# First batch's routing drawn forward, more of its row transfers in the first program, six matmuls left out

## The chip, the cores and the metric

One core of one Trainium2 chip. The time is device microseconds (us) of one launch. The kernel before ran in 748.58 us, the median of three runs (748.47 to 749.82).

## The reference, cut to what matters

One transformer block over x of 2 batches x 1024 tokens x 256, in float32:

```python
h = layernorm(x) * (1 + ca) + sa                 # ca, sa, ga, ... from silu(c) @ wmod, per batch
x = x + ga * attention(h)                        # 32 heads of 8, 8 key heads, causal softmax, then @ wo
h = layernorm(x) * (1 + cb) + sb
probs = softmax(h @ w_router)                    # 16 experts
top_w, top_i = top_k(probs, 4); top_w /= sum(top_w)
moe = sum over the 4 chosen e of top_w[e] * (silu(h @ we1[e]) * (h @ we3[e])) @ we2[e]      # H = 128
shared = (silu(h @ ws1) * (h @ ws3)) @ ws2                                                  # 512 wide
x = x + gb * (shared / 5 + moe * 4 / 5)
```

## The kernel before, in words

The kernel is two programs one after the other. Each is a block of instruction lists, one for each engine, and an engine starts the second block only when all engines have come to the end of the first.

**The first program** makes the projections and then the attention in 16 groups (batch x key head), each in 10 steps (`STEPS`, s = 0 to 9). TensorE (PE) computes the scores of step s in one or two slots into PSUM banks (L1264), ScalarE (ACT) takes their exponentials (L1047, L1052), GpSimd (POOL) zeroes what the causal mask hides in the steps s = 0, 1, 2, 7, 8, 9 (L871), and PE multiplies with the values two steps later (`product`, L1283). VectorE (DVE) works out row maxima for the group after (L1453 and others). They end in group 14 of 0 to 15, since the maxima run ahead; in the rest of group 14 and in group 15 DVE is free.

The first batch (groups 0 to 7) is out of the attention early, so its second half is laid into the groups of the other batch: output projection in group 13 (`output_pair`), layernorm moments after it, and, once DVE has done its last maxima, `normal(1)`, `normal(2)` (L212). From there `first_batch(group, s)`, called at the end of each step of PE's list, places: `turned_x(1)`, `turned_x(2)` (transposes, L518) after steps 6 and 7 of group 14, `router(1)`, `router(2)` (logits, L534) after steps 8 and 9 of it, and `ranks` (two products that count hits per expert, L280 and L281) after step 4 of group 15. DVE makes from the transposed rows `h2` (L1533), its high part `h2_hi` (L1536) one column block at a time, and its low part (L1541), then the routing (`Routing`): `logits` (L240, L241), a wait for ACT's exponential of the logits (L1031, placed ahead of step 1 of group 15), `best`, `best_at`, `chosen`, `counted` (L248 to L266: it releases `ranks`), `weights`, and, once `ranks` is done, `totals`, `firsts`, `places`, which end with the row positions `posi` (L309, semaphore `pos_ready`).

Every token's row goes to 4 sorted places in memory: 32 indirect transfers (`scatter(pool, 0, k)`, 128 rows each, L549) issued by POOL. Transfer 0 stands ahead of the mask of step 8 in group 15 (`AMONG`), 1 to 7 behind the mask of step 9, some behind waits (`spread`, `att_full`, `up1_full`) that pace them, and 8 to 31 at the start of the second program.

After the attention's last product PE does `reciprocals`, `output(3)` (L577) and `up(0)`, `up(1)`, the first two products of the shared expert (L605), and the first program ends.

**The second program.** SP starts the loads of all experts' weights (`w_all`, L1613 and L1614), and behind them, once all 32 transfers have landed (`sorted_s[0]`), the loads of the sorted rows by tiles of 128 (L1622). PE goes through `reciprocals(4)`, `output(4)`, `down(0)` to `down(3)` (L1796), `up(2)` to `up(4)`, `turned_x(3)` and `(4)`, `router(3)` and `(4)` (L534), then six products of the identity that nobody reads (L1869), and then the loop over 94 tiles: `turned_rows` (L1809), `up_rows` (L1830), `turned_g` (L1841), `down_rows` (L1847). `turned_rows(0)` waits for the first tile's load and for DVE's `shared_mult(4)` (L1907). ACT's list ahead of the loop ends with `high(4)` (L1707), the exponential of the second batch's logits (L1760) and one small Silu (L1762) that brings the table for the loop; then come `shifted_rows(0)` and `(1)` (L1729). Behind the loop is the rest of the shared expert, and the outputs.

The order on each engine is written out by hand. There is no planner.

## Time and profile before

| | |
|---|---|
| median of three runs | 748.58 us |
| span of the profiled execution (first to last instruction) | 745.6 us, 3.0 us under that median |
| PE busy | 696.8 us, 93% |
| DVE, ACT, POOL busy | 72%, 66%, 37% |
| mean granted TensorE clock | 0.972 of full |
| POOL, 32 transfers of the first batch's rows (L549) | 30.7 us, 959 ns each |

All times are on the profile's own clock, from the first instruction. A busy engine can still be waiting in effect: PE has 93% here, and what counts is where it stands idle and what it then waits for. The attention ends near 478 us and the first program near 487.9 us. Of the granted clock, 1.00 is 2.4 GHz and 0.50 is 1.2 GHz.

### The profile page before, as it was taken

The numbers are of one execution on the slowest core, as the hardware profiler recorded it, in microseconds if no ns is written. First come the engines' busy times: TensorE is split into PE (matmuls) and PEld (weight loads), VectorE is DVE, ScalarE is ACT, GpSimd is POOL, SyncE is SP. The second block draws the span as 40 slices with busy tenths as digits, with TensorE's granted clock in tenths as the row PEclk, the third lists the DMA queues.
The fourth block names the chain that finished last, engine by engine and source line by source line (L and its number), as shares of the span: only waits on it lengthen the run. The fifth ranks groups of instructions, "written<-read, shape, count | busy, mean of one in ns | idle before, by whom it ended". The sixth has DMA issues, their size and how long they took to land. (4 is left out here: it accounts for less than half of the span.)

```text
span 745.6 us, 14744 instructions
## 1 busy us (share of the span) xinstructions
PE 696.8 (93%) x4960; PEld 441.5 (59%) x4960; DVE 539.0 (72%) x1159; ACT 493.6 (66%) x739; POOL 272.2 (37%) x332
## 2 busy tenths in 40 slices
PE   8989899999999999999999888897899999999994
PEld 7447544444445444444444434577678888887883
DVE  7846988888888888888887775456395556775477
ACT  4341579999898988899888477345556666664232
POOL 5702104433323222233332112567016706540772
PEclk9998989999999999999999999997799999999999
DMA  7755603455453554543443000387447758873342
GB/s 234 204 119 148 183 5 105 116 161 166 156 167 100 162 159 142 161 106 103 116 124 87 1 19 30 110 267 254 128 148 249 267 178 235 245 235 129 92 140 79
DMA packets 78580, 108.71 MB, mean 146 GB/s; under 512 B 16200, under 2 KB 60040, under 8 KB 77420
## 3 DMA queue, kind: packets, MB, share of 16 engines
q1 hardware_dynamic: 67996, 77.16, 35.6%
q0 software_dynamic: 9280, 29.11, 12.1%
q10 hardware_dynamic: 1232, 1.51, 0.7%
q8 instruction: 42, 0.69, 0.4%
q14 instruction: 30, 0.25, 0.1%
HBM read 59.92 MB, written 47.39 MB: 144 GB/s over the span
## 5 line engine op out<-in xcount | busy, mean ns | idle before, releaser
L1052 ACT ACTIVATE probs<-psum 128x1024 f32<-128x1024 f32 x256 | 246.6, 1027 | 47.2 <-PE psum L1264 46.7
L1453 DVE TENSOR_REDUCE max_parts<-psum 128x2 f32<-128x1024 f32 (+2 forms) x160 | 196.0, 1225 | 68.1 <-PE psum L1200 66.3
L871 POOL TENSOR_SCALAR_AFFINE_SELECT probs<-probs 128x512 f32<-128x512 f32 (+1 forms) x96 | 79.2, 826 | 221.1 <-ACT probs L1052 201.5
L1283 PE MATMUL psum<-probs,v_aug 128*32 128x512 f32 (+3 forms) x1536 | 158.9, 501 | 0.3 <-POOL probs L871 0.2
L1264 PE MATMUL psum<-qs,ks 64*128 64x512 f32 (+3 forms) x768 | 136.2, 394 | 11.5 <-ACT over L978 5.0
L1264 PEld LDWEIGHTS psum<-qs,ks 64*128 64x128 f32 x768 | 65.8, 186 | 109.7 <-ACT probs L1052 69.0
L1830 PE MATMUL psum<-w_all,v_aug 128*128 x376 | 98.7, 386 | 0.7 <-ACT v_aug L1729 0.6
L1200 PE MATMUL psum<-km,qs 64*128 64x128 f32 (+2 forms) x608 | 75.6, 322 | 8.4 <-DVE max_parts L1453 4.2
L1729 ACT ACTIVATE v_aug<-psum,modc 128x128 f32<-128x128 f32 x188 | 75.7, 453 | 4.9 <-PE psum L1809 4.6
L1830 PEld LDWEIGHTS psum<-w_all,v_aug 128*128 128x128 f32 x376 | 71.9, 193 | 11.6 <-issue 2.0
L1283 PEld LDWEIGHTS psum<-probs,v_aug 128*32 128x32 f32 x1536 | 34.0, 109 | 65.5 <-issue 61.2
L1927 DVE TENSOR_TENSOR v_aug<-v_aug,psum 128x128 f32<-128x128 f32 x94 | 27.0, 287 | 60.7 <-ACT v_aug L1737 60.6
L1212 PE MATMUL psum<-km,qs 64*128 64x512 f32 x160 | 66.0, 413 | 0.4 <-DVE max_parts L1472 0.2
L1737 ACT ACTIVATE v_aug<-psum 128x128 f32<-128x128 f32 x94 | 26.0, 277 | 58.3 <-PE psum L1830 58.3
L1200 PEld LDWEIGHTS psum<-km,qs 64*128 64x128 f32 x608 | 51.1, 187 | 19.1 <-DVE max_parts L1453 10.3
L1847 PE MATMUL psum<-w_all,v_aug 128*128 x188 | 56.5, 383 | 0.0
L978 ACT ACTIVATE over<-psum 128x1024 f32<-128x1024 f32 x48 | 49.3, 1026 | 10.5 <-DVE max_parts L1472 5.1
L1659 POOL DMA_INDIRECT h_t<-y_sorted,posi x32 | 31.5, 985 | 55.3 <-PE psum L605 23.7
L549 POOL DMA_INDIRECT x_sorted<-probs,posi x32 | 30.7, 959 | 46.5 <-DVE posi L309 34.3
L1472 DVE CUSTOM_DVE_ANT_0 psum<-psum,over 128x512 f32<-128x512 f32 x64 | 44.2, 691 | 0.0
L1809 PE MATMUL psum<-ident,late 128*128 128x128 f32 x188 | 36.8, 279 | 6.5 <-DMA late<-x_sorted 6.5
L1940 DVE TENSOR_TENSOR late<-psum,gate 128x256 f32<-128x256 f32 x94 | 39.5, 421 | 1.2 <-PE psum L1847 1.0
(200 smaller groups left out, 1014.6 us busy)
## 6 DMA issues: line engine op xcount, KB each, us to landing
late<-x_sorted SPq DMA_DIRECT2D x94, 128.0 KB, 2.8
y_sorted<-late SPq DMA_DIRECT2D x94, 128.0 KB
x_sorted<-g_rows POOLq DMA_DIRECT2D x6, 1536.0 KB, 7.4
qs<-q_parts SPq DMA_DIRECT2D x62, 128.0 KB
km<-k_parts SPq DMA_DIRECT2D x62, 96.0 KB
km<-k_parts SPq DMA_DIRECT2D x64, 64.0 KB
ks<-k_parts SPq DMA_DIRECT2D x64, 64.0 KB
y_sums<-g_sign SPq DMA_DIRECT2D x16, 256.0 KB, 2.7
```

The lines of the kernel that those rows point to most:

```text
L871: pool.affine_select(out=tile, in_=tile, compare_op=ALU.is_ge, fill=0.0, base=0, pattern=[[0, REP], [0, n], [1, P]], channel_multiplier=-1 ...
L978: act.activation(to, psum[:, banks, :], ACT.Relu).then_inc(over_done, 1)
L1052: act.activation(to[:, 2 * slot:2 * slot + 2, off:TT], psum[:, banks, off:TT], ACT.Exp, scale=SCALE).then_inc(p_full, 1)
L1200: last = pe.matmul(bank[wide_bank + hp][:, k * w:(k + 1) * w], qs[buf][rows, hh, i * P:(i + 1) * P], km[buf][rows, at:at + w], start=(k == ...
L1212: pe.matmul(bank[narrow_bank][:], qs[buf][rows, hh, i * P:(i + 1) * P], km[buf][rows, KU:KU + TT], start=True, stop=True).then_inc(narrow_ ...
L1264: last = pe.matmul(bank[first + hp][:, to:to + width], ks[buf][rows, c * P:(c + 1) * P], qs[buf][rows, hh, half * TT + off:(half + 1) * TT ...
L1283: last = pe.matmul(bank[sum_bank][32 * h:32 * h + 32, off:TT], v_aug[:, at:at + 32], probs[(NSTEP * group + s) % (LAG + 1)][:, h, col:col ...
L1453: dve.tensor_reduce(out=max_parts[:, :, h0:h1, slice(*tiles), slot], in_=psum[:, wide_bank:wide_bank + 2, :].rearrange("p a (s w) -> p (a ...
L1472: dve.tensor_tensor_reduce(out=bank[narrow_bank][:], in0=bank[narrow_bank][:], in1=over[:, hp, :], scale=1.0, scalar=LEAST, op0=ALU.add, o ...
L1729: last = act.activation(xt[:, k % 2, c * P:(c + 1) * P], bank[X_BANKS[k % 2]][:, c * P:(c + 1) * P], ACT.Identity, scale=modc[:, b, 1, c, ...
L1830: last = pe.matmul(bank[U_BANKS[k % 2]][:, 0:2 * H], xt[:, k % 2, c * P:(c + 1) * P], w_all[:, bass.ds(expert[k], 1), c * 2 * H:(c + 1) * ...
L1847: pe.matmul(bank[Y_BANKS[k % 2]][:, 0:D], gt[:, k % 2, :], w_all[:, bass.ds(expert[k], 1), W13:WCOLS].rearrange("p a n -> p (a n)"), start ...
```

## The change

Seven edits:

1. On PE, `turned_x(1)`, `turned_x(2)`, `router(1)`, `router(2)` stand one step earlier in group 14 (after steps 5, 6, 7, 8), and `ranks` after step 0 of group 15 instead of step 4. `router` for the first batch waits for `xt2_read`, which counts the `h2` pieces, and the semaphore `h2_dve` is gone.
2. On DVE the high part is made for 1024 columns at a time (`high_parts`), once ahead of the logits and once ahead of `best`; the low part (`low_parts`) moves behind `places`.
3. ACT's exponential of the first batch's logits stands between the two slots of step 9 in group 14.
4. POOL's transfers 0 to 4 stand ahead of the mask of step 7 of group 15, transfer 5 ahead of that of step 8, and 6 to 14 behind the mask of step 9, with the waits that 1 to 7 had.
5. In the second program 17 transfers are left (15 to 31) instead of 24, and the waits between them are dealt out anew; the last four come behind `down_done` 2.
6. The six identity products (L1869) are gone.
7. A semaphore less is allocated.

```diff
@@ -424,8 +424,8 @@
         wo_done, yn_pool, yn_dve, att_full = sem("wo_gated_done"), sem("yn_by_pool"), sem("yn_by_dve"), sem("att_full")
         var2, sqrt2, xn2_done = sem("var2_ready"), sem("sqrt2_done"), sem("xn2_done")
         resid, xt2_full, xt2_read = sem("residual_done"), sem("xt2_full"), sem("xt2_read")
-        h2_dve, h2_act, hi_dve, hi_act, h2_lo_s, h2_lo1_s = [sem(n) for n in (
-            "h2_by_dve", "h2_by_act", "h2_high_by_dve", "h2_high_by_act", "h2_low_done", "h2_low1_done")]
+        h2_act, hi_dve, hi_act, h2_lo_s, h2_lo1_s = [sem(n) for n in (
+            "h2_by_act", "h2_high_by_dve", "h2_high_by_act", "h2_low_done", "h2_low1_done")]
         lg_full = sem("logits_full")
         lg_banks = 6, 5
 
@@ -522,7 +522,7 @@
         def router(pe, n):
             half, to = (n - 1) % 2, bank[lg_banks[(n - 1) // 2]]
             if n <= 2:
-                pe.wait_ge(h2_dve, DC * n)
+                pe.wait_ge(xt2_read, DC * n)
                 if n == 1:
                     pe.wait_ge(narrow_free, NPAIR * GROUPS)
             else:
@@ -537,8 +537,8 @@
 
         sorted_s = [sem(f"x_sorted_{b}") for b in range(B)]
 
-        AMONG = {8: (0,)}
-        SCATTERED = 8
+        AMONG = {NSTEP - 3: range(5), NSTEP - 2: range(5, 6)}
+        SCATTERED = 15
 
         def scatter(pool, b, k):
 
@@ -906,16 +906,17 @@
                             pool.wait_ge(y_in[n], 64)
                             pool.tensor_tensor(out=y_t[0][:, n], in0=y_t[0][:, n], in1=r_t[:, n], op=ALU.mult).then_inc(yn_pool, 1)
 
-                scatter(pool, 0, 1)
+                scatter(pool, 0, 6)
                 for m in range(DC):
                     pool.wait_ge(spread, m + 1)
-                    scatter(pool, 0, 2 + m)
-                scatter(pool, 0, 4)
+                    scatter(pool, 0, 7 + m)
+                scatter(pool, 0, 9)
                 pool.wait_ge(att_full, 5)
-                scatter(pool, 0, 5)
-                scatter(pool, 0, 6)
+                scatter(pool, 0, 10)
+                scatter(pool, 0, 11)
                 pool.wait_ge(up1_full, 1)
-                scatter(pool, 0, 7)
+                for k in range(12, SCATTERED):
+                    scatter(pool, 0, k)
 
             @block.scalar
             def _(act):
@@ -1026,9 +1027,6 @@
                     for s, (half, blocks, n) in enumerate(STEPS):
                         if group == GROUPS - 2 and s == 3:
                             square_roots(act, 0, var2, sqrt2)
-                        if group == GROUPS - 1 and s == 1:
-                            act.wait_ge(lg_ready, 1)
-                            act.activation(route[0].lg, route[0].lg, ACT.Exp).then_inc(lg_exp, 1)
                         if NSTEP * group + s > LAG:
                             act.wait_ge(pv_done, NSTEP * group + s - LAG)
                         if NSTEP * group + s == LAG:
@@ -1036,6 +1034,9 @@
                         to = probs[(NSTEP * group + s) % (LAG + 1)]
                         for slot in range(3 if (s, 2) in DIFF_AT else 2):
                             banks = banks_of(group, s, slot)
+                            if group == GROUPS - 2 and s == NSTEP - 1 and slot == 1:
+                                act.wait_ge(lg_ready, 1)
+                                act.activation(route[0].lg, route[0].lg, ACT.Exp).then_inc(lg_exp, 1)
                             if (s, slot) in DIFF_AT:
                                 which, ahead = DIFF_AT[s, slot]
                                 if group + ahead < GROUPS:
@@ -1304,11 +1305,11 @@
 
                     if group == OUT_GROUP and OUT_STEP <= s < OUT_STEP + 4:
                         output_pair(s - OUT_STEP)
-                    elif group == GROUPS - 2 and s in (6, 7):
-                        turned_x(pe, s - 5)
-                    elif group == GROUPS - 2 and s in (8, 9):
-                        router(pe, s - 7)
-                    elif group == GROUPS - 1 and s == 4:
+                    elif group == GROUPS - 2 and s in (5, 6):
+                        turned_x(pe, s - 4)
+                    elif group == GROUPS - 2 and s in (7, 8):
+                        router(pe, s - 6)
+                    elif group == GROUPS - 1 and s == 0:
                         route[0].ranks(pe, bank[lg_banks[0]][:, 2 * P:4 * P])
 
                 pe.wait_ge(v_done, 2)
@@ -1532,19 +1533,24 @@
                         dve.wait_ge(xt2_full, k)
                         dve.tensor_scalar(h2[:, n - 1, c, :], bank[T_BANKS[n - 1][c]][:], modc[:, 0, 1, c, 0:1],
                                           modc[:, 0, 1, c, 1:2], ALU.mult, ALU.add).then_inc(xt2_read, 1)
-                        dve.wait_ge(xt2_read, k)
-                        dve.tensor_copy(h2_hi[0][:, c, toks], h2[:, n - 1, c, :]).then_inc(hi_dve, 1)
-                        dve.sem_inc(h2_dve, 1)
-                for n in (1, 2):
+
+                def high_parts(n):
+                    toks = slice((n - 1) * TT, n * TT)
+                    dve.wait_ge(xt2_read, DC * n)
+                    dve.tensor_copy(h2_hi[0][:, :, toks], h2[:, n - 1]).then_inc(hi_dve, DC)
+
+                def low_parts(n):
                     toks = slice((n - 1) * TT, n * TT)
                     dve.wait_ge(hi_dve, DC * n)
                     dve.tensor_tensor(out=h2_lo[0][:, :, toks], in0=h2[:, n - 1], in1=h2_hi[0][:, :, toks].bitcast(F32),
                                       op=ALU.subtract).then_inc(h2_lo_s, 1)
 
+                high_parts(1)
                 dve.wait_ge(lg_full, 2)
                 route[0].logits(dve, chain.link, bank[lg_banks[0]][:, 0:P].rearrange("p (j e) -> p j e", e=E))
 
                 ranked = bank[lg_banks[0]][:, 2 * P:4 * P]
+                high_parts(2)
                 route[0].best(dve, chain.link)
                 route[0].best_at(dve, chain.link, range(TC))
                 route[0].chosen(dve, chain.link)
@@ -1553,6 +1559,8 @@
                 route[0].totals(dve, chain.link, ranked, range(TC))
                 route[0].firsts(dve, chain.link, ranked)
                 route[0].places(dve, chain.link)
+                for n in (1, 2):
+                    low_parts(n)
                 late_reciprocals(dve, 0)
                 spread_sums(dve, 0)
                 residual(dve, chain.link, 3)
@@ -1664,33 +1672,20 @@
                     for k in some:
                         scatter(pool, 0, k)
 
-                scatters(8, 9)
+                scatters(15, 16)
                 for m in range(DC):
                     pool.wait_ge(spread, DC + m + 1)
-                    scatters(10 + 2 * m, 11 + 2 * m)
+                    scatters(17 + 2 * m, 18 + 2 * m)
                 pool.wait_ge(up1_full, 3)
-                scatters(14, 15)
+                scatters(21, 22)
                 pool.wait_ge(up3_full, 3)
-                scatters(16, 17)
+                scatters(23, 24)
                 pool.wait_ge(att_full, 6)
-                scatters(18)
+                scatters(25)
                 pool.wait_ge(down_done, 1)
-                scatters(19, 20)
+                scatters(26, 27)
                 pool.wait_ge(down_done, 2)
-                scatters(21)
-                pool.wait_ge(up1_full, 4)
-                scatters(22)
-                pool.wait_ge(up3_full, 4)
-                scatters(23)
-                pool.wait_ge(down_done, 3)
-                scatters(24, 25)
-                for c in range(2 * DC):
-                    pool.wait_ge(xt2_full, 2 * DC + c + 1)
-                    scatters(26 + c)
-                pool.wait_ge(up1_full, 5)
-                scatters(30)
-                pool.wait_ge(up3_full, 5)
-                scatters(31)
+                scatters(28, 29, 30, 31)
                 for k in range(ROUTES):
                     if k:
                         pool.wait_ge(u_full, ROUTED_AT + 4 * k // 5)
@@ -1865,8 +1860,6 @@
                 router(pe, 4)
 
                 pe.wait_ge(hi_act, 2 * DC)
-                for _ in range(6):
-                    pe.matmul(bank[Y_BANKS[1]][:, 0:P], ident[:], ident[:], start=True, stop=True)
                 for i in range(-AHEAD_T, NTILE + 2):
                     if 0 <= i < NTILE:
                         up_rows(i)
```

## Rows read from the trace of the kernel before

**Rows 1.** The chain of waits, 487 to 526 us: start us, us, what.

```profile
519.71 2.39 DMA x_sorted<-xn,posi
...
522.12 2.03 DMA late<-x_sorted
```

**Rows 2.** The waits, 485 to 530 us: us in total, times, longest.

```profile
PE psum L1809 <- DMA late<-x_sorted: 6.5, 1, 6.5
```

**Rows 3.** The timeline of ACT: start us, us, what, [idle before <-releaser].

```profile
518.94 1.28 ACT L1762 ACT_TABLE_LOAD   x1
520.23 0.20 ACT L1762 ACTIVATE v_aug<-sd 128x1 f32<-128x1 f32 x1
524.92 1.50 ACT L1729 ACTIVATE v_aug<-psum,modc 128x128 f32<-128x128 f32 x4 [4.49 <-PE psum L1809]
```

**Rows 4.** The timeline of DVE in the second program.

```profile
515.96 0.68 DVE L1907 TENSOR_TENSOR wmod_sb<-wmod_sb,psum 128x512 f32<-128x512 f32 x1
```

**Rows 5.** The timeline of PE, the identity products.

```profile
514.82 2.91 PE L1869 MATMUL psum<-ident 128*128 128x128 f32 x12
```

**Rows 6.** The timeline of PE in groups 14 and 15.

```profile
440.96 0.50 PE L1264 MATMUL psum<-qs,ks 64*128 64x512 f32 x2 [0.41 <-ACT probs L1052]
...
449.41 0.79 PE L1264 MATMUL psum<-qs,ks 64*128 64x384 f32 x8
...
451.12 1.96 PE L534 MATMUL psum<-wr_sb,h_t 128*128 128x16 f32 x16
...
453.67 0.64 PE L1283 MATMUL psum<-probs,v_aug 128*32 128x256 f32 x8
...
462.56 0.49 PE L280 MATMUL psum<-wmod_sb,g_rows 128*128 128x128 f32 x2
```

**Rows 7.** The timeline of ACT in groups 14 and 15.

```profile
450.01 1.94 ACT L1052 ACTIVATE probs<-psum 128x1024 f32<-128x1024 f32 x2 [2.29 <-PE psum L1264]
...
455.43 0.31 ACT L1031 ACTIVATE g_rows<-g_rows 128x128 f32<-128x128 f32 x1
455.63 1.02 ACT L1047 ACTIVATE probs<-psum 128x1024 f32<-128x1024 f32 x1
...
463.80 3.77 ACT L1052 ACTIVATE probs<-psum 128x1024 f32<-128x1024 f32 x4 [0.40 <-PE psum L1264]
```

**Rows 8.** The timeline of DVE, the first batch's routing.

```profile
453.12 0.29 DVE L240 TENSOR_REDUCE g_rows<-psum 128x8 f32<-128x128 f32 x1 [2.15 <-PE psum L534]
...
455.89 0.71 DVE L248 MAX8 wmod_sb<-g_rows 128x8 f32<-128x16 f32 x8 [2.15 <-ACT g_rows L1031]
...
459.20 1.07 DVE L266 TENSOR_REDUCE wmod_sb<-wmod_sb 128x128 f32<-128x512 f32 x1
...
469.49 0.18 DVE L309 CAST posi<-wmod_sb 128x32 uint32<-128x32 f32 x1
```

**Rows 9.** The timeline of POOL at the end of the first program.

```profile
481.99 0.96 POOL L549 DMA_INDIRECT x_sorted<-xn,posi  x1 [2.18 <-PE psum L577]
...
488.51 0.96 POOL L549 DMA_INDIRECT x_sorted<-xn,posi  x1 [3.04 <-POOLq L634]
```

**Rows 10.** The timeline of PE across the two programs.

```profile
486.68 0.63 PE L605 MATMUL psum<-km,w_hi 128*128 128x512 f32 x2
488.91 2.05 PE L588 MATMUL psum<-k_parts_sb 128*128 128x128 f32 x16 [1.60 <-DVE k_parts_sb L612]
```

**Rows 11.** Stretches: us, PE, PEld, DVE, ACT, POOL busy (x), granted clock, DMA share, GB/s.

```profile
432.30:434.50 2.20, 0.06 (x6) 0.01 (x2) 0.94 (x3) 2.19 (x3) 0.00 (x0) 1.00 0.00 0
434.50:438.50 4.00, 4.00 (x25) 1.51 (x27) 2.85 (x8) 2.76 (x3) 0.33 (x2) 0.57 0.00 0
...
488.90:492.00 3.10, 3.09 (x22) 2.87 (x23) 1.51 (x3) 1.97 (x4) 2.49 (x3) 1.00 0.93 281
...
733.50:735.80 2.30, 0.10 (x2) 0.08 (x1) 1.60 (x4) 1.43 (x3) 0.00 (x0) 1.00 0.00 0
735.80:738.00 2.20, 1.61 (x12) 1.41 (x12) 2.06 (x6) 0.00 (x0) 0.00 (x0) 1.00 0.00 0
```

## The prediction

> **What bounds the kernel now.** I read the page first (busy shares, the granted clock by slices), then the chain that ended last, then the waits around the place where the chain leaves TensorE, and last the timelines of the engines there. PE is busy for 93% of the span, so the question is where it is not. The chain runs back from the end through the tile loop, all on PE, to one handover: the last indirect transfer of sorted rows starts on POOL at 519.71, lands 2.39 us later, the first tile's load takes 2.03 more, and PE's first transpose starts at 524.20 [rows 1]. The waits show that PE stood 6.5 us for that load [rows 2], the longest idle time in the whole trace. Ahead of it POOL is the chain: from 488.51 on it issues transfers 8 to 31 without a pause, 0.96 us each and 0.30 between, some of them slower. So the change aims at a real bound. How much it is worth depends on who is late next.
>
> **The change part by part.** I work on the profile's clock. Its span, 745.6, lies 3.0 under the median of the three runs, 748.58; I take differences and add them to the median.
>
> *The second program's transfers, 17 instead of 24.* At 1.26 us each, the seven that go would bring the last landing from 522.1 to 513 or before, and PE's other work ends at 514.82, where the identity products begin [rows 5]. If only transfers, tile load and PE counted, the loop would start near 515 and the gain would be 9 us. But two other lists end later. `turned_rows(0)` also waits for `shared_mult(4)` on DVE, which runs from 515.96 to 516.64 [rows 4]. And ACT, which must shift tile 0 before PE can multiply it, is still in its old list: the table load of the last Silu starts at 518.94 and the Silu itself ends at 520.43 [rows 3]. In the trace ACT's first shift is at 524.92 [rows 3]; after the change it is at 520.45 at the earliest, as everything in ACT's list up to there hangs on PE's and DVE's work and not on the transfers. The loop can therefore gain 524.92 − 520.45 = 4.5 us, half of the 9. Ends: 0, if the transfers, which then run wholly beside the weight loads, land only at 522; and 4.5, for the reason given. I take 4.5, since 17 transfers from 488.51 end by 510 to 511 and even a slow landing leaves several us.
>
> The Trainium skill (ScalarE: Activation LUTs, "What ACT_TABLE_LOAD costs") says that a switch of tables costs a drain of about the load's own length on top of the load. The trace has the Silu at 520.23, 0.01 behind the end of the load [rows 3], so nothing of the kind is seen at this switch. By the page, an ACT list with two switches would end 2.8 us later and the gain be 1.7; I follow the row.
>
> *The identity products.* They end at 517.73 and PE idles until 524.20 anyway [rows 2, 5]; the clock was at half all through them. What they hid is nothing; taken away they free PE for `turned_rows(0)`, which is ready at 516.7. Zero, with ends −0.5 and +0.5 (when the clock comes back after the restart).
>
> *The routing in groups 14 and 15.* `turned_x(1)` now fills PE's wait of 0.41 before 440.96 [rows 6]. `router(2)` comes ahead of step 9, so from 451.12 − 1.71 (the step that starts at 449.41 [rows 6]) − 0.4 and some tenths of overlap I put its start at 448.8 and the logits on DVE, which started 2.00 behind it [rows 6, 8], at 450.8. `lg_ready` is then at 451.4. ACT's exponential stands behind slot 0 of step 9. That slot started at 450.01 [rows 7]; behind `router(2)` instead of ahead of it, it starts at 451.2 and ends at 452.15. So the exponential is at 452.15, not 455.43 [rows 7], and doesn't wait. From exponential to `best` it was 0.46, and from `best` to the end of `counted` 459.20 + 1.07 − 455.89 = 4.4 [rows 8]. `hits_s` thus comes at 452.15 + 0.46 + 4.4 = 457.0. The two `high_parts` (0.9 each, an estimate from a cast of 512 columns at 0.43) fall into waits of DVE. `low_parts` are off every path there.
>
> Now the waiting place. PE used to come to `ranks` at 462.56 [rows 6], two us after `hits_s` at 460.3; it waited for nothing. In the new list `ranks` stands behind step 0 of group 15, whose product ended at 454.3 [rows 6] and will end at about 454.45 (0.6 of PE work less ahead of it, but slot 1 of its scores now waits for ACT's slot 1 of step 9, which the exponential pushed to 453.35). PE then stands 457.05 − 454.45 = **2.6 us** in front of `ranks`, and behind it in the list are the scores of step 1, for which ACT waits. Step 1 reaches ACT at 457.7 (end of `ranks`) + 0.5 = 458.2; it was 455.63 [rows 7]: +2.6. Of this 0.4 comes back at step 5, where `ranks` no longer delays the scores (ACT's idle 0.40 before 463.80 [rows 7]). From there to the end of the attention PE and ACT hand each other the work, ACT with hardly a gap, so that nothing more is regained: **+2.15 us** at the attention's end. Ends: +1.2 (`hits_s` an us sooner) and +3.2.
>
> *Transfers 0 to 4.* `posi` was written 469.49 − 462.56 = 6.9 us behind `ranks` [rows 6, 8]; now that is at 464.0. Five transfers from 464.2 at 1.26 to 1.6 us end at 470.5 to 472.2. The mask of step 7, behind them on POOL, could start at 470.2 and with the shift of 2.15 at 472.3. It isn't held up: 0, upper end +0.5. Transfer 5 stands where transfer 0 stood.
>
> *The end of the first program.* Transfer 10 waits for `att_full` 5 as transfer 5 did, at 481.99 [rows 9]. Then come five instead of two before the barrier: the last begins at 481.99 + 4 x 1.26 = 487.03 and ends at 487.99. PE's last product ends at 486.68 + 0.63 = 487.31 [rows 10]. So POOL takes PE's place as the last to arrive, by 0.7, or 1.0 with the 0.30 behind an issue. **+0.8 us**, between 0.4 and 1.2; all of the second program starts later by this. In the list behind it PE has no idle time from 488.91 on, so nothing absorbs it.
>
> Sum without the clock: −4.5 + 2.15 + 0.8 = **−1.5 us** (−1.55 rounded), 747.0.
>
> *The clock.* Both new waits touch it. After an idle time of 2.14 us in group 14 (PE busy 0.06 of 2.20) the granted clock was 0.57 in the 4.0 us behind it [rows 11]: 4.0 x 0.43 = 1.7 us of full-rate work lost. After 1.60 us between the programs [rows 10] it stayed 1.00 [rows 11], and after some 2.2 us near 733 too. So such a gap takes the clock sometimes. The stall in front of `ranks` (2.6 us, call it A) is in the attention, where the gap of 2.14 did; its price is 1.7, less some tenths that ACT hides: 1.4. The gap between the programs grows from 1.6 to 2.4 (B), and there PE is the bound and the price is the full 1.7. I hold A for more likely than not, B for even.
>
> The Trainium skill (TensorE: Matmul & The Clock Gate, "HAM oscillation") names as dangerous only gaps longer than any of these; by it neither A nor B would cost anything and the sum stays −1.5. The gap of 2.14 us with half clock behind it [rows 11] speaks against it, and the one near 733 for it.
>
> **The rivals.**
>
> 1. *Forecast: stall, later barrier and A.* −1.5 + 1.4 = −0.15: 748.4 us. No change that can be measured (0.2%, 1.5 us, is about what a measurement of this kernel can tell).
> 2. *A and B.* The wait in front of `ranks` and the longer gap both take the clock: −1.5 + 1.4 + 1.7 = +1.6, 750.1 us, slower. It decides from the point where POOL's end at the barrier makes PE's gap over two us. For it: 2.14 was enough once. Against: 1.60 in this very place wasn't, and 2.2 near 733 wasn't.
> 3. *No gap takes the clock* (what the page's rule gives too): 747.0 us, just faster.
> 4. *The stall in front of `ranks` isn't there*, because `hits_s` comes before PE or ACT has work in store: −4.5 + 0.8 and up to 0.4 lost or won: 744.9 us. Against it: from the exponential to `counted` are 4.9 us of DVE work in series, and PE has 2.3 us of work between the two.
> 5. *The transfers stay the bound* (slower ones beside the weight loads, landing at 522): 748.58 + 2.15 + 0.8 + a clock gap or two: 752 us.
>
> **How the numbers follow.** Chances: case 1 0.34, case 2 0.24, case 3 0.18, case 4 0.13, case 5 0.05, else 0.06. Around each lies ±0.7 for the phase of the clock in the rest. Faster by over 0.2% (under 747.1): most of case 4, over half of case 3 and a little of 1, 0.33. Slower (over 750.1): half of case 2, case 5, part of 1 and of the rest, 0.27. Within: 0.40. The range 745.2 to 750.9 leaves out the far half of case 4, case 5 and the edge of case 2. Case 1 alone: 747.4 to 749.3.
>
> **What would show it.** In the timeline of PE: an idle time of 2 to 3 us in front of L280 at 454 to 457, released by DVE L266, and then a clock of 0.5 to 0.6 for some us (A). POOL's last transfer in the first program ending after PE's last L605, and DVE's first instruction of the second program 0.4 to 1.2 later behind it (barrier). The first L1729 directly behind the Silu L1762, and PE's wait in front of the loop no longer put down to a DMA. Wrong if L280 starts without a wait, if the mask of step 7 waits for a transfer, or if the first L1809 still waits for x_sorted.

## The result, and the profile after

| | us | ratio to the kernel before |
|---|---|---|
| kernel before, four runs | 749.20 median (748.47 to 749.95) | |
| changed kernel, four runs | 753.33 median (752.28 to 754.48) | 1.0059, 95% interval 1.0038 to 1.0081 |
| forecast | 748.4 (745.2 to 750.9) | |

The changed kernel is slower by 4.1 us, beyond the range. The profiled execution took 753.34, with a span of 751.0 against 745.6. I cut both spans at five events of PE:

| stretch | before | after | difference |
|---|---|---|---|
| start to the first score behind the gap in group 14 | 434.49 | 436.01 | +1.5 |
| from there to output(3) (L577) | 43.53 | 48.39 | +4.9 |
| from there to the second program's first L588 | 10.89 | 13.74 | +2.85 |
| from there to the end of the last router product | 26.07 | 26.90 | +0.8 |
| from there to the first `up_rows` | 10.95 | 7.07 | −3.9 |
| from there to the end | 219.6 | 218.9 | −0.7 |

The 1.5 us in the first row lie in code that the change doesn't touch, and in the traces of the later runs this point falls anywhere from 433.3 to 437.6, so I count them as no part of its price. The other rows give +3.9.

The chain that ended last, in order of time (start us, us, what). It no longer contains a transfer of sorted rows [rows 1]; between the programs it goes over one DVE instruction, and at the loop's start over ACT's table loads.

```profile
497.13 0.96 DVE k_parts_sb L612
498.09 0.04 issue
498.14 3.07 PE psum L588 x16
...
528.09 1.28 ACT L1755
529.38 0.01 issue
529.39 0.31 ACT g_rows L1755
529.70 0.02 issue
529.71 1.28 ACT L1757
```

PE's timeline at the three places. The first answers to the 462.56 of [rows 6], the second to [rows 10], the last two to [rows 1, 2]:

```profile
455.51 0.64 PE L1284 MATMUL psum<-probs,v_aug 128*32 128x256 f32 x8
459.11 0.80 PE L280 MATMUL psum<-wmod_sb,g_rows 128*128 128x128 f32 x2 [2.96 <-DVE wmod_sb L266]
...
493.06 0.64 PE L605 MATMUL psum<-km,w_hi 128*128 128x512 f32 x2
498.14 2.22 PE L588 MATMUL psum<-k_parts_sb 128*128 128x128 f32 x12 [4.44 <-DVE k_parts_sb L612]
...
527.56 1.08 PE L1804 MATMUL psum<-ident,late 128*128 128x128 f32 x4 [2.52 <-DVE wmod_sb L1900]
532.11 2.07 PE L1825 MATMUL psum<-w_all,v_aug 128*128 x4 [3.47 <-ACT v_aug L1724]
```

PE waits 2.96 us for the hits; it waited for nothing there before. It waits 4.44 between the programs instead of 1.60. And at the loop the wait of 6.5 us for the DMA is gone. What stands in its place, as forecast, is `shared_mult(4)` and then ACT's list: the first shift follows the Silu with nothing between, where before there were 4.5 us of waiting [rows 3].

```profile
529.71 1.28 ACT L1757 ACT_TABLE_LOAD   x1
531.01 0.20 ACT L1757 ACTIVATE v_aug<-sd 128x1 f32<-128x1 f32 x1
531.12 1.49 ACT L1724 ACTIVATE v_aug<-psum,modc 128x128 f32<-128x128 f32 x4
```

POOL's timeline. Transfers 0 to 4 do not hold up the mask of step 7; the second pair of lines answers to [rows 9]:

```profile
473.11 0.96 POOL L549 DMA_INDIRECT x_sorted<-xn,posi  x1 [0.30 <-issue]
476.62 0.67 POOL L871 TENSOR_SCALAR_AFFINE_SELECT probs<-probs 128x512 f32<-128x512 f32 x1 [2.55 <-ACT probs L1053]
...
493.43 0.96 POOL L549 DMA_INDIRECT x_sorted<-xn,posi  x1 [0.30 <-issue]
497.73 0.96 POOL L549 DMA_INDIRECT x_sorted<-xn,posi  x1 [3.34 <-POOLq L634]
```

The first thing that another engine does behind the barrier between the programs is a table load of ACT, first before, then after:

```profile
487.87 1.28 ACT L1713 ACT_TABLE_LOAD   x1 [11.15 <-PEq L634]
```

```profile
497.09 1.28 ACT L1708 ACT_TABLE_LOAD   x1 [14.00 <-PEq L634]
```

And two stretches with the columns of [rows 11], behind the two waits: the clock is at its lower level (0.5, 1.2 GHz) in both, after 2.96 and after 4.44 us without a product.

```profile
458.00:465.00 7.00, 5.89 (x40) 3.26 (x40) 5.79 (x25) 2.88 (x4) 0.69 (x1) 0.51 0.09 35
498.90:502.30 3.40, 3.40 (x16) 3.11 (x15) 2.59 (x5) 1.78 (x4) 2.70 (x3) 0.51 1.00 296
```

### The profile page after: what moved, and what is told of

It is laid out like the page before. It is cut to its first block and busy times, and to the rows that moved or that the text cites. A ratio compares the mean times of both kernels' runs of the same rounds, so it can differ in the third digit from the quotient of the medians.

```text
span 751.0 us, 14717 instructions
## 1 busy us (share of the span) xinstructions
PE 698.3 (93%) x4948; PEld 441.5 (59%) x4948; DVE 539.7 (72%) x1157; ACT 494.0 (66%) x739; POOL 271.1 (36%) x332
## 5 line engine op out<-in xcount | busy, mean ns | idle before, releaser
L1053 ACT ACTIVATE probs<-psum 128x1024 f32<-128x1024 f32 x256 | 246.9, 1028 | 50.4 <-PE psum L1265 49.9
L1284 PE MATMUL psum<-probs,v_aug 128*32 128x512 f32 (+3 forms) x1536 | 161.3, 508 | 0.4 <-POOL probs L871 0.4
L1265 PE MATMUL psum<-qs,ks 64*128 64x512 f32 (+3 forms) x768 | 139.5, 403 | 12.5 <-ACT over L979 5.0
L1265 PEld LDWEIGHTS psum<-qs,ks 64*128 64x128 f32 x768 | 68.1, 192 | 111.3 <-ACT probs L1053 67.3
L1201 PE MATMUL psum<-km,qs 64*128 64x128 f32 (+2 forms) x608 | 77.2, 328 | 6.9 <-DVE max_parts L1454 2.9
L1825 PEld LDWEIGHTS psum<-w_all,v_aug 128*128 128x128 f32 x376 | 71.6, 193 | 14.8 <-issue 5.0
L979 ACT ACTIVATE over<-psum 128x1024 f32<-128x1024 f32 x48 | 49.2, 1026 | 10.6 <-DVE max_parts L1473 5.1
L1048 ACT ACTIVATE probs<-psum 128x1024 f32<-128x1024 f32 x32 | 32.9, 1027 | 15.4 <-PE psum L1265 15.1
```

The costliest lines, as they stand in the source:

```text
L979: act.activation(to, psum[:, banks, :], ACT.Relu).then_inc(over_done, 1)
L1053: act.activation(to[:, 2 * slot:2 * slot + 2, off:TT], psum[:, banks, off:TT], ACT.Exp, scale=SCALE).then_inc(p_full, 1)
L1201: last = pe.matmul(bank[wide_bank + hp][:, k * w:(k + 1) * w], qs[buf][rows, hh, i * P:(i + 1) * P], km[buf][rows, at:at + w], start=(k == ...
L1265: last = pe.matmul(bank[first + hp][:, to:to + width], ks[buf][rows, c * P:(c + 1) * P], qs[buf][rows, hh, half * TT + off:(half + 1) * TT ...
L1284: last = pe.matmul(bank[sum_bank][32 * h:32 * h + 32, off:TT], v_aug[:, at:at + 32], probs[(NSTEP * group + s) % (LAG + 1)][:, h, col:col ...
L1825: last = pe.matmul(bank[U_BANKS[k % 2]][:, 0:2 * H], xt[:, k % 2, c * P:(c + 1) * P], w_all[:, bass.ds(expert[k], 1), c * 2 * H:(c + 1) * ...
```

## The experiments

Two cautions for reading them. All ran on other chips than the first pair, where the kernel before itself took 769 to 772 us (single runs from 762 to 776), so each ratio carries ±0.3% or so and means little alone. Their traces show where the time goes. Engines stand still in the second program ahead of the tile loop, which the first two traces don't show (below). And the part from the first `up_rows` to the end, 219 and 220 us in the first two traces, is 231 to 237 there, in all kernels; that is the larger part of the 20 us, it varies by 4 us between two traces of one kernel (e7), and what makes it was not looked into. What the traces say of the stretches in the first program is steadier (the changed kernel's stretch in the attention was 47.2 to 48.4 in four traces, its gap 13.7 in all), so the verdicts on the stalls rest on stretches. The last four rows are runs with held loads, described at the end of this section; every ratio is to the unchanged kernel before on the same chip.

| kernel | ratio (95%) | gap in group 14 to output(3) | output(3) to first L588 | PE idle, first L588 to last router | last router to first up_rows | first up_rows to the end |
|---|---|---|---|---|---|---|
| before (first chip) | | 43.5 | 10.9 | 0.1 | 10.95 | 219.6 |
| changed (first chip) | 1.0059 (1.0038, 1.0081) | 48.4 | 13.7 | 0.3 | 7.1 | 218.9 |
| changed, again | 1.0020 (0.9984, 1.0056) | 47.2 | 13.7 | 4.2 | 6.3 | 235.2 |
| changed, third | 0.9991 (0.9968, 1.0015) | 47.8 | 13.7 | 4.2 | 5.2 | 234.3 |
| e1 ranks after 2 | 0.9992 (0.9958, 1.0025) | 44.7 | 13.7 | 3.0 | 7.1 | 233.6 |
| e2 twelve | 1.0007 (0.9969, 1.0045) | 49.0 | 10.6 | 6.8 | 7.1 | 233.6 |
| e3 identity back | 1.0013 (0.9981, 1.0044) | 48.5 | 13.7 | 2.6 | 6.45 | 236.9 |
| e4 routing alone | 1.0047 (1.0006, 1.0089) | 48.95 | 10.9 | 7.2 | 9.8 | 232.9 |
| e5 three more | 1.0033 (0.9993, 1.0072) | 43.3 | 14.8 | 1.5 | 10.1 | 234.5 |
| e6 ranks 2, eleven | 0.9943 (0.9910, 0.9976) | 43.2 | 10.6 | 8.5 | 7.0 | 232.5 |
| e6 again | 0.9936 (0.9907, 0.9965) | 42.95 | 10.6 | 8.9 | 6.8 | 230.9 |
| e7 and logits first | 0.9954 (0.9920, 0.9988) | 43.0 | 10.6 | 9.0 | 5.3 | 231.9 |
| e7 again | 0.9924 (0.9892, 0.9956) | 43.0 | 10.6 | 8.9 | 5.4 | 236.2 |
| e8 ranks 2, eight | 0.9991 (0.9960, 1.0022) | 43.2 | 10.9 | 5.4 | 7.8 | 234.2 |
| e9 gap filled | 1.0052 (1.0021, 1.0082) | 48.6 | 15.9 | 4.3 | 6.2 | 234.5 |
| e12 reciprocals first | 0.9955 (0.9919, 0.9990) | 43.0 | 9.6 | 9.8 | 5.4 | 233.4 |
| e13 before, held | 1.0015 (0.9981, 1.0049) | 43.5 | 10.9 | 6.3 | 9.7 | 234.9 |
| e14 changed, held | 0.9988 (0.9957, 1.0018) | 47.8 | 13.7 | 4.3 | 5.1 | 231.2 |
| e15 eleven, held | 0.9966 (0.9939, 0.9993) | 43.0 | 10.6 | 8.9 | 7.0 | 231.0 |
| e16 logits, held | 0.9943 (0.9913, 0.9973) | 44.7 | 10.6 | 8.2 | 5.6 | 231.3 |

**The stall in front of the rank products (e1).**

```diff
-                    elif group == GROUPS - 1 and s == 0:
+                    elif group == GROUPS - 1 and s == 2:
                         route[0].ranks(pe, bank[lg_banks[0]][:, 2 * P:4 * P])
```

> The changed kernel with one edit: PE's two rank products stand after step 2 of group 15, not after step 0. Theory S (the 2.96 us that PE waited for DVE L266, and the half clock behind that wait, are on the path): the wait goes (hits are ready when PE comes there), the half clock behind it too, some 4.5 us; the five transfers ahead of the mask of step 7 start about 1.5 us later against that mask and hold it up by 1 to 1.5. So 3 to 3.5 us less than the changed kernel, about 750. Theory R (the wait is slack that the attention gives back, and the loss is elsewhere, at the end of the first program): no more than 1 us less, about 752.5 to 753.3.

PE's timeline of e1 shows the wait gone:

```profile
458.21 1.07 PE L1284 MATMUL psum<-probs,v_aug 128*32 128x512 f32 x8
459.21 0.49 PE L280 MATMUL psum<-wmod_sb,g_rows 128*128 128x128 f32 x2
```

The stretch to output(3) is 44.7 instead of 47.2 to 48.4: 2.5 to 3.7 us less, as theory S had it. It isn't back at 43.5 because transfers 0 to 4 now start later against the attention and hold up the mask of step 7, also as expected: POOL's mask starts at 473.16, straight behind transfer 4. With three transfers there instead of five (e6) it is 43.2. The total shows less of it than expected: 769.87 against 771.36 for the changed kernel on the same chip, 1.5 us less where 3 to 3.5 were expected. So the stall with its half clock cost 4.0 to 5.4 us in the changed kernel's traces, of which 2.96 is the wait.

**The routing drawn forward, alone (e4).** The changed kernel with the transfers and the identity products of the kernel before.

```diff
-        AMONG = {NSTEP - 3: range(5), NSTEP - 2: range(5, 6)}
-        SCATTERED = 15
+        AMONG = {8: (0,)}
+        SCATTERED = 8
...
```

> The changed kernel with the transfers placed as in the kernel before (8 in the first program, 24 in the second, the old waits) and the six identity products back: only the routing is drawn forward. Theory S: the attention ends 4 to 5 us later (2.96 of waiting for the hits, half clock behind it, 0.4 back), the gap between the programs is 1.6 us as before, and POOL's transfers behind it are the bound as before, so all of it stays: 753 to 754, four to five over the kernel before. Theory R (the loss is at the program's end): 749 to 750.

+5.4 us in the attention and nothing between the programs: 1.0047, 3.6 us. The interval only just clears 1, and the expectation that the transfers are the bound at the loop isn't borne out by this trace: PE's first transpose there (536.24) waits for DVE's `shared_mult(4)`, and the last transfer had started at 527.58. The stall alone is in the trace as expected; that it alone makes a kernel slower rests on this one ratio.

**The end of the first program (e2, e5).** e2 is the changed kernel with 12 transfers in the first program:

```diff
-        SCATTERED = 15
+        SCATTERED = 12
...
-                scatters(15, 16)
+                scatters(*range(12, 17))
```

> The changed kernel with 12 instead of 15 transfers in the first program (the three behind the wait for up1 move to the start of the second). Theory S (POOL comes to the end of the first program 2.2 to 2.5 us behind its last transfer's end, so three transfers more make the barrier 2.8 us later, and the gap on PE takes the clock): POOL's last transfer there ends 3.8 us earlier, PE is the last to arrive, its gap between the programs is 1.5 us instead of 4.4, no half clock behind it: 2.8 + 1.5 = 4 us less, about 749. The 20 transfers left end well ahead of ACT's readiness. Theory R (the loss is all in the attention): the same as the changed kernel within 1 us.

e5 is the kernel before with three more:

```diff
-        SCATTERED = 8
+        SCATTERED = 11
...
                 pool.wait_ge(up1_full, 1)
-                scatter(pool, 0, 7)
+                for k in range(7, SCATTERED):
+                    scatter(pool, 0, k)
...
```

> The kernel before with one edit: 11 instead of 8 transfers in the first program, the three more behind its last. Theory D (POOL comes to the end of the first program some 3.3 us behind the start of its last transfer, whatever stands around it, and in the kernel before it is level with PE there): the second program starts 3.6 to 3.8 us later against output(3), PE's gap is 5.3 us, and a half clock may follow. The transfers stay serial, so the last one lands where it did or an us later; 1 to 3 us slower than before. Rival (as the prediction had it: POOL is free 0.3 us behind its last transfer, so PE sets the end until POOL's last transfer ends later): PE's gap grows by 2.0 us only, to 3.6.

PE's first product of the second program, first in e2, then in e5:

```profile
495.70 2.05 PE L588 MATMUL psum<-k_parts_sb 128*128 128x128 f32 x16 [1.33 <-DVE k_parts_sb L612]
```

```profile
494.33 2.93 PE L588 MATMUL psum<-k_parts_sb 128*128 128x128 f32 x12 [5.52 <-DVE k_parts_sb L612]
```

Three transfers fewer take 3.1 us from the gap, and the half clock behind it goes too (2.05 for the sixteen products instead of 3.07); three more put 3.9 to it. The rival with a tail of 0.3 us foretold a gap of 3.6, and the gap is 5.52. The totals don't carry this. e2 is level with the changed kernel on the same chip (771.22 and 771.36) where 4 us less was expected; in its trace the attention is 1.8 longer than in the changed kernel's and the stretch behind the gap 1.6. e5 is at 1.0033, with 1 in its interval.

POOL arrives last in eleven traces, and in all of them the other engines start again 3.4 to 3.7 us behind the *start* of POOL's last transfer: 484.51 and 487.87 before, 493.43 and 497.09 after, 489.81 and 493.29 in e5, 485.85 and 489.23 in e8. The traces also record the drain with which each engine ends the program (L634). POOL's ends 3.1 to 3.4 us behind the start of its last transfer in every trace, whether POOL is last or not: at 487.62 before and 496.85 after, against 487.36 and 493.74 for PE's. The others start 0.25 us behind the later of the two. In e2 that is PE's, at 494.41; POOL's took 3.24 from 490.36 on. So POOL was last in the kernel before already, by 0.26 us. Whether the drain waits for the landing (2.4 us behind the start) or for POOL's own work was not told apart.

**The two mended together (e6), and the gain by itself (e8).** e6 has the rank products after step 2, transfers 0 to 2 ahead of the mask of step 7 and 3 ahead of that of step 8, and 11 in the first program.

```diff
-        AMONG = {NSTEP - 3: range(5), NSTEP - 2: range(5, 6)}
-        SCATTERED = 15
+        AMONG = {NSTEP - 3: range(3), NSTEP - 2: range(3, 4)}
+        SCATTERED = 11
...
```

> The changed kernel with both terms taken out: rank products after step 2 of group 15, transfers 0 to 2 ahead of the mask of step 7 and 3 ahead of that of step 8, 11 in the first program so that the last one ends where the last of 8 ended before. Theory S: attention as long as before, gap of 1.6 us as before, tile loop led by ACT's Silu: the 4.5 us at the loop's start are left as a gain, 744.5 to 746, faster than both kernels. Theory R (the gain of 4.5 at the loop's start is given back later in any case): 748 to 749.

> The kernel with the rank products after step 2 and 11 transfers in the first program, a second time, beside the changed kernel. Theory S: 0.4 to 0.6% faster than the kernel before, 1.0 to 1.2% faster than the changed one. Theory R (what was gained was this kernel's luck with stalls while the expert weights are loaded): within 0.2% of the kernel before.

0.9943 and 0.9936: by the ratios 4.4 and 4.9 us faster than the kernel before (3.4 and 4.2 by the medians), both intervals clear of 1. On the chip where the changed kernel ran beside it, that one took 771.36 and this one 765.00. Its two stretches in the first program are those of the kernel before or some tenths shorter, so both stalls are out, and what is left is a gain, as theory S had it. That it is the gain at the loop's start isn't shown on these chips, as the next run says.

e8 is the same early routing with 8 transfers, placed as before, and the identity products.

> Routing drawn forward as in the changed kernel but with the rank products after step 2 of group 15, and all transfers as in the kernel before. Theory S: attention and gap as before, and as the transfers are the bound again, the loop starts where it did: the same as the kernel before within 0.2%. Beside the kernel with 11 transfers, which was 0.6% faster, this says that the gain is that of the transfers. Rival (the earlier routing itself makes the gain): 0.4% faster or more.

0.9991, as foretold: in the total, earlier routing shows no gain without the transfers behind it, within ±0.3%. The trace doesn't say the same so plainly. PE's first transpose waits for the transfers there (3.74 us for the first tile's load), as it should, but the first `up_rows` comes 94.4 us behind the gap in group 14, sooner than in e6 (96.4 and 96.7), since PE stands idle for 5.4 us ahead of it and not for 8.5 to 8.9 (the still-stands described below). So the totals of e8 and e6 fit theory S, though their intervals touch, and the rival named for e6, that its gain lies in where the still-stands fall, isn't excluded.

**The identity products (e3)** back in the changed kernel:

```diff
+                for _ in range(6):
+                    pe.matmul(bank[Y_BANKS[1]][:, 0:P], ident[:], ident[:], start=True, stop=True)
```

> The changed kernel with the six products of the identity back in front of the tile loop. Every term as in the changed kernel; the products stand in front of the first transposes, which wait for shared_mult(4) anyway. Theory: 0, as the loop starts with ACT's list. Rival: the products hold the clock up, so that the half clock at the loop's start is shorter, 0.5 to 1.5 us faster.

1.0013 against 1.0020 and 0.9991 without them, on other chips: no difference that this can show. The clock was at half in the stretch from the last router product to the first `up_rows` with them (0.50), so they did not hold it up.

**What sets the loop's start (e7).** e6 with DVE's logits of the second batch ahead of `shared_mult(4)`, and ACT's exponential and Silu ahead of `high(4)`.

```diff
-                high(FRONT)
                 act.wait_ge(lg_ready, 2)
                 act.activation(route[1].lg, route[1].lg, ACT.Exp).then_inc(lg_exp, 1)
 
                 act.activation(tm[:, 1, 0:1], sd[:, 0:1], ACT.Silu)
+                high(FRONT)
...
```

> The kernel with the rank products after step 2 and 11 transfers, and one edit more: the second batch's logits, their exponential and the small Silu come ahead of the shared expert's mult(4) and high(4) on DVE and ACT. Theory L (ACT's list ahead of the loop sets when the loop starts): first tile shifted 1.0 to 1.5 us sooner, 1 to 1.5 us less than the same kernel without this edit. Rival: the loop waits for the load of sorted rows or for the weights just behind, and nothing is gained.

> The kernel with rank products after step 2, 11 transfers and the logits first, again. Without the still-stands: about 743, 0.8% faster than the kernel before (4.5 us of the loop's start, 1.6 of the logits). With them: 0.4 to 0.6% faster.

ACT's timeline in e7:

```profile
529.14 0.31 ACT L1755 ACTIVATE g_rows<-g_rows 128x128 f32<-128x128 f32 x1 [2.57 <-DVE g_rows L241]
529.47 1.28 ACT L1757 ACT_TABLE_LOAD   x1
530.76 0.20 ACT L1757 ACTIVATE v_aug<-sd 128x1 f32<-128x1 f32 x1
530.87 0.61 ACT L1703 ACTIVATE km<-wmod_sb 128x512 fp32r<-128x512 f32 x1
531.39 1.49 ACT L1725 ACTIVATE v_aug<-psum,modc 128x128 f32<-128x128 f32 x4
```

The stretch from the last router product to the first `up_rows` is 5.3 and 5.4 instead of 6.8 to 7.0: 1.5 us sooner, so ACT's list is what the loop waits for. In the total it doesn't show beside e6 (0.9954 and 0.9924 against 0.9943 and 0.9936). It never met a chip without still-stands, so its 743 us were not tried.

**The gap and its clock (e9).** 24 identity products behind PE's last product of the first program of the changed kernel.

```diff
+                pe.wait_ge(y_done, GROUPS + 1)
+                for _ in range(24):
+                    pe.matmul(bank[sum_bank][:, 0:P], ident[:], ident[:], start=True, stop=True)
```

> The changed kernel with 24 products of the identity behind PE's last product of the first program (0.13 us each at full clock for a pass, some 3 us), which fill the gap between the programs and delay nothing, since POOL comes later there. What the half clock behind that gap costs: theory S says 1.5 us (23.26 us instead of 21.71 for PE's work from the first L588 to the last L534), so 1 to 1.5 us less than the changed kernel. Rival: the clock behind the gap is not on the path, 0.

```profile
493.47 5.52 PE L1368 MATMUL psum<-ident 128*128 128x128 f32 x48
500.29 1.94 PE L588 MATMUL psum<-k_parts_sb 128*128 128x128 f32 x15 [1.30 <-DVE k_parts_sb L612]
```

The experiment didn't do what it was made for: each product is recorded as two matmuls of 0.115 us, so that they took 5.5 us, not 3, and made the second program 2.2 us later themselves. The clock did stay up (1.94 for the products that took 3.07), but the price of the half clock can't be read from the total.

**The last DVE instruction in the gap (e12).** e7 with `late_reciprocals(dve, 1)` moved from the start of the second program to the end of the first.

> The kernel with rank products after step 2, 11 transfers and the logits first, and one edit more: DVE's late_reciprocals(1) stands at the end of the first program instead of the start of the second, so that PE finds them ready. PE's gap between the programs is 1.33 us with it behind the barrier, of which 0.96 is this instruction and some 0.1 its waits; it should be 0.3 to 0.5. One us less than without this edit, 0.6 to 0.8% faster than the kernel before. Rival: PE then waits for something else at the start of the program (its code, or the rows of sums), and nothing is gained.

```profile
490.03 2.02 PE L588 MATMUL psum<-k_parts_sb 128*128 128x128 f32 x16 [0.32 <-PEq L634]
```

The gap is 0.32, one us less, as expected; the total, 0.9955, shows nothing of it beside e7.

**The same two kernels elsewhere, and held loads.** Since the first ratio didn't repeat, the changed kernel ran twice more.

> The changed kernel itself, so that the others of this chip have it beside them. Every theory: 0.4 to 0.8% slower than the kernel before; in the trace 2.9 to 3.0 us of waiting in front of the rank products and 4.4 between the programs.

> The changed kernel a third time, on whatever chip it meets. If the engines don't stand still between 500 and 517: 0.4 to 0.8% slower than the kernel before. If they do: within 0.4% of it, since a start of the second program that is 5 to 8 us later then meets a shorter still-stand.

1.0020 and 0.9991. The first was expected at 1.004 to 1.008 by every theory, so the loss of the first pair didn't repeat in the total; the second is within what was expected with still-stands. In these traces the stall (2.95) and the gap (4.44) are as in the first. What differs is behind them. In e6 (its second run) PE and ACT stand still in the second program; first PE's row, then ACT's, and then the row of PE at this place in a later run (e15, below) in which the profile names the releaser:

```profile
510.12 2.07 PE L1792 MATMUL psum<-w_hi,km 128*128 128x256 f32 x8 [8.09 <-issue]
```

```profile
508.71 0.63 ACT L1703 ACTIVATE km<-wmod_sb 128x512 fp32r<-128x512 f32 x1 [16.14 <-remote]
```

```profile
511.10 2.07 PE L1794 MATMUL psum<-w_hi,km 128*128 128x256 f32 x8 [8.12 <-DVE km L1907]
```

PE waits for DVE's `low(2)`, which waits for ACT's `high(2)`, the instruction at 508.71. And that one waits for PE's `down(0)` (semaphore `down_done`). The product is recorded as ended at 497.82, but the semaphore as raised only at 508.62, 10.8 us later, and ACT starts 0.09 behind it. In the first pair's traces such a semaphore comes 0.02 behind the product (509.46 and 509.48 after). In the changed kernel on these chips the waiter is another, the wait the same: DVE's L565 waits until 508.31 for a product of PE (L577) that is recorded as ended at 504.36. So a still-stand is a time in which PE's signals come late; since the profile models the ends of matmuls, the traces don't tell whether the products themselves ran late or only the signals. Why it happens on these chips and not on the first is open.

PE's idle time between the first L588 and the last router product is 8.5 to 8.9 us in e6, 6.8 in e2, 4.2 in the changed kernel on these chips, and 0.3 on the first. It doesn't simply shrink when the program starts later: e2 and e4 start as late as the changed kernel (first L588 at 495.7 and 495.8 against 494.5 and 496.2) and stand 6.8 and 7.2, while e8 starts at 490.3 and stands 5.4. It goes with the kernel: two traces of one kernel agree within 0.5 us. To weaken a suspected cause, four kernels held the last quarter of the expert weights' loads back:

```diff
                 for q in range(E // 4):
+                    if q == 3:
+                        sp.wait_ge(xt2_full, 2 * DC + 1)
```

> The kernel before with one edit: SP holds the last quarter of the expert weights' loads back until PE's turned_x(3) is done. In the traces of most of the runs so far engines stand still for 1 to 16 us, released by nothing that the profile shows, between 500 and 517, while the weights are loaded, and not in the first two traces. Theory C (the loads keep engines from their next instructions): the still-stands shrink, several us faster where they were. Rival (they have another cause): the same, or slower by what the loads come later.

> The changed kernel with the same held loads. Against the kernel before with held loads. Theory C, with stall, barrier and clock as they were read: 4 to 5 us slower than it (0.5 to 0.6%), the price in the first two traces. Rival (the price is really 0.2%, and the first figure was the chip's): 1 to 2 us slower.

> The kernel with the rank products after step 2 and 11 transfers, with held loads. Theory: 4 to 5 us faster than the kernel before with held loads, as the tile loop then starts with ACT's list and neither stall is there. Rival (the gain was in where the still-stands fell): 0 to 1 us.

> The same with the second batch's logits first, with held loads. Theory L (ACT's list sets the loop's start): another 1 to 1.6 us faster. Rival: the same as without them, since what is gained at the loop's start is lost in the half clock behind it.

1.0015 (0.9981 to 1.0049) for the kernel before, 0.9988 (0.9957 to 1.0018) for the changed one, 0.9966 (0.9939 to 0.9993) for e6 and 0.9943 (0.9913 to 0.9973) for e7, all against the kernel before without the edit. PE still stood 8.1 us in the latter two, and its idle time is 4.3 in the changed kernel and 8.9 in e6, as without the edit. So holding this quarter doesn't shorten the still-stand. It is a weak test of theory C, though: the other three quarters were still loading through it (DMA busy 0.88 from 503.0 to 509.7 in e15, where ACT goes on at 509.7). The cause stays open.

One of the four expectations was missed outright. The changed kernel was to be 4 to 5 us slower than the kernel before with the same edit, or 1 to 2 by the rival; its median is 3.7 us lower (767.99 against 771.69; by the means 2.2, ±2.2). e6 is 3.9 below the kernel before, near what was expected, but level with the changed kernel (767.76), which on another chip it had beaten by 6.4. e7 is 1.2 below e6, within the noise of ±2 us.

The traces of the first two show where the loss of the change goes on such a chip. Stall and gap are there in full: 47.8 against 43.5 and 13.7 against 10.9, together 7.2 us. But from the first L588 to the first `up_rows` the changed kernel gains 7.3 (from 45.0 to 37.7) and not 3.0 as on the first chip (from 37.0 to 34.0), since PE stands still for less and DVE doesn't stand for 10.12 us ahead of `shared_mult(4)` as it does in the kernel before. The first `up_rows` comes 99.3 us behind the gap in group 14 in the changed kernel and 99.5 in the kernel before, where the first chip has 96.1 and 91.4. In e6 it comes at 96.4 to 96.7.

## Why the prediction was wrong

- *The tile loop's start, −4.5.* Right. The transfers ceased to be the bound, ACT's Silu took their place, the first shift stands 0.11 behind its start; e7 confirms it. Measured −3.9 on the first chip, and −0.7 behind the first `up_rows`, which was not forecast. Less than half of what the transfers alone would have given, as worked out.
- *The stall in front of `ranks`, +2.15, and case A, +1.4.* The wait was forecast with 2.6 and is 2.96. `hits_s` came 0.3 us later against the rest, the L261 group taking 1.38 instead of 0.90 beside a mask of POOL. The clock fell, as held likely, but for 6.8 us where the model for its price [rows 11] was half as long. Together +4.9 where 3.55 (2.15 + 1.4) was forecast. The mechanism was right, the size of A was not.
- *The later barrier, +0.8.* This is the step that failed: "**+0.8 us**, between 0.4 and 1.2". It measured +2.85. I took POOL as arrived at the end of its last transfer's row, or 0.30 later. But the row at 488.51 [rows 9] ends 3.04 us of POOL's idle time, and the other engines start 2.4 us behind the end of the last transfer's record. POOL was last, by 0.26, already in the kernel before, where I had PE last and POOL with 1.8 us to spare. So every transfer more behind `att_full` costs its whole pace of 1.26, not only what reaches beyond PE's end. "Five instead of two" is a slip: the kernel before has three there (5, 6 and 7). Two more make 2.5 us, and POOL's drain was 0.3 longer, together the 2.85. e2 and e5 show it in both directions (−3.1, where PE becomes the last, and +3.9).
- *Case B.* With a gap of 4.4 us and not 2.4 it wasn't even chances; the clock fell in this trace and in all others with that gap except the filled one. The half clock behind the gap lasted 3.4 us, which is the full 1.7 of the forecast; it cost 1.0 alone in the first sixteen products (3.07 against 2.05). The stretch shows only 0.8 since in the kernel before it was its end that ran at half clock: 4.36 us for the last router products, against 3.64 after. That was not foreseen.
- *The identity products, 0.* Right within what e3 can tell.
- *The Trainium skill.* Of ScalarE: Activation LUTs, the drain beside a table load ("What ACT_TABLE_LOAD costs") is again not seen: the load at 529.71 starts as the exponential ends (529.39 + 0.31), it ends at 530.99, and the Silu starts at 531.01. Of TensorE: Matmul & The Clock Gate, the warning under "HAM oscillation" against long gaps would cover the gap of 4.44 us as it came. It doesn't cover the stall: 2.96 us was enough there.

So the case that came is case 2, with the barrier mis-sized by 2.05 us and A by 1.3: 750.1 + 2.05 + 1.3 = 753.5, less the 0.9 by which B was overpriced, and plus 0.6, by which the median of before lies higher in the four runs: 753.2, against 753.33 measured. That this is so close is partly luck. It leaves out what nobody forecast: +0.6 at the loop's start, −0.7 behind it, +1.5 ahead of the gap in group 14, and −0.7 since the profiled run after lies only 2.3 above its span and not 3.0; these come to +0.7, which the sum needs from the profiled run of before, 748.58, in place of the 0.6. The range failed since the bound of the barrier term, 1.2, was taken from a row's end and not from the idle time behind it, and A added 1.3.

What stays open: on the chips with still-stands the change costs −0.1 to 0.2% (0.9991 and 1.0020), within noise, and the reason for these is unknown. The four us of the first chip are measured on that chip alone. The stall and the gap are shown everywhere, their price in the total only there.

## What to carry to other kernels

When an engine's last work before a barrier issues transfers, read its arrival from when the *others* start again, not from the end of its last row: here 3.4 to 3.7 us behind the start of the last transfer. A step drawn forward in an in-order list wants its consumer placed by when its input is ready: the rank products in front of their input took 4.0 to 5.4 us, as much as the whole gain, and two steps later, with three transfers and not five ahead of the mask, they took nothing. When one engine's queue is the bound, list who else must be ready at the same place before pricing the gain; the second latest took half of it.

## What the runs showed of the hardware that was not expected

- With an indirect transfer as POOL's last work, the other engines got past the barrier 3.4 to 3.7 us behind that transfer's start, in eleven traces; POOL's drain ended 3.1 to 3.4 behind it in all. In e2 it is recorded with 3.24.
- The clock fell to half within the wait or up to 1.3 us behind it after 2.95 us without a product in the attention, in all eight traces that have that gap, for 3.4 or 6.8 us.
- The same program takes 749 us on one chip and 769 to 772 on the others. There PE stands idle 1.5 to 9.8 us in the second program ahead of the loop, as its semaphores are raised up to 11.0 us (e12) behind the recorded ends of its products, where the first chip has 0.02. The length goes with the kernel. 11 to 18 us more lie behind the first `up_rows`, unexplained.
